# An MLP over sixteen token tiles, worked in five blocks of 2, 4, 4, 4 and 2 tiles instead of four blocks of 4

## The reference

```
hs = layernorm(x)                                 # H=512 channels of C=4
o  = attention(rat_read(hs, attn_read_w, 3))
hs = rat_write(hs, o, attn_wod_w, attn_wab_w, attn_du_w)       # "a" of a tile
mlp_in = rat_read(hs, mlp_read_w, 2)              # 2 x 512 per token, normalised
gate = mlp_in[..., :H] @ mlp_in_w[0].T            # 512 -> M=2048
up   = mlp_in[..., H:] @ mlp_in_w[1].T            # 512 -> 2048
y = silu(gate) * up
hs = rat_write(hs, y, mlp_wod_w, mlp_wab_w, mlp_du_w)          # "w" of a tile
x = x + hs
x = x + low_rank_experts(layernorm(x))                         # "e" of a tile

def rat_write(res, y, ...):       # 632 outputs: 512 out, 8 delta_low, 112 gates
    out, delta_low, A_logit, B_proj, B_skip = y @ [wod; wab].T
    delta = softplus(delta_low @ du_w.T)
    A_bar = exp(-delta * softplus(A_logit))
    return res * A_bar + out * B_full(A_bar, delta, B_proj, B_skip)
```

## Time and profile before

| | us |
|---|---|
| median of 3 runs (1856.93 to 1860.12) | 1858.18 |
| the profiled execution, its own time | 1859.11 |
| its span in the trace | 1857.3 |
| mix stage: from 643.6 to the end | 1213.7 |
| of it, before the first up step | 119.8 |
| the four blocks | 246.0, 290.0, 272.5, 212.4 |
| after the last down step | 73.0 |
| PE busy, whole span | 1648.2 |
| DVE busy, whole span | 1173.0 |

### The profile page before, as it was taken

One profiled execution on the slowest core, in us unless ns is written; L12 is line 12 of the kernel. 1 busy time (PEld: TensorE's weight loads), 2 busy tenths in 40 slices (PEclk: granted clock), 3 DMA queues, 4 the chain that ended last, 5 costly groups with the idle time before them and its releaser, 6 DMA issues.

```text
span 1857.3 us, 23597 instructions
## 1 busy us (share of the span) xinstructions
PE 1648.2 (89%) x8854; PEld 1138.3 (61%) x8854; DVE 1173.0 (63%) x1873; ACT 794.4 (43%) x1486; POOL 267.6 (14%) x243
## 2 busy tenths in 40 slices
PE   6799999999999866899898999897999998999865
PEld 5565655666666535677566677455677565775543
DVE  6678755888888657254355647637458455555577
ACT  1333336888887634455224444223444322331221
POOL 1235332334320000200002000003000002000000
PEclk7899999999999976799898999998999999999988
DMA  7376567878775252566473666554565544665721
GB/s 301 114 266 239 209 172 232 242 205 243 213 195 119 71 203 96 187 223 205 147 236 127 228 214 202 173 164 169 190 234 196 191 161 149 222 200 173 252 79 68
DMA packets 117221, 348.69 MB, mean 188 GB/s; under 512 B 16226, under 2 KB 33250, under 8 KB 101876
## 3 DMA queue, kind: packets, MB, share of 16 engines
q1 hardware_dynamic: 117108, 347.19, 57.6%
HBM read 271.37 MB, written 75.76 MB: 187 GB/s over the span
## 4 chain that ended last, share of the span: by engine, by line
PE 65%; DVE 22%; ACT 6%; issue 4%; DMA 1%; POOL 1%; SPq 0%; DVEq 0%; ACTq 0%
PE ps L1365 15%; PE ps L1377 11%; PE ps L396 6%; PE ps L820 4%; PE ps L1280 4%; PE ps L807 4%; PE ps L843 4%; PE ps L1323 3%; PE ps L1265 3%; PE ps L1308 3%; ACT a_p L922 3%; PE ps L1335 2%; DVE m_A L1438 2%; PE ps L369 2%; DVE m_A L1469 2%
## 5 line engine op out<-in xcount | busy, mean ns | idle before, releaser
L1365 PE MATMUL ps<-m_yhi,m_win 128*128 128x512 f32 x1024 | 352.9, 413 | 0.0
L1377 PE MATMUL ps<-m_wod,m_hT 128*128 128x512 f32 (+1 forms) x1024 | 312.2, 454 | 8.0 <-DVE m_hT L1563 8.0
L1377 PEld LDWEIGHTS ps<-m_wod,m_hT 128*128 128x128 f32 x1024 | 173.6, 201 | 152.0 <-issue 151.5
L1365 PEld LDWEIGHTS ps<-m_yhi,m_win 128*128 128x128 f32 x1024 | 195.4, 191 | 49.2 <-issue 5.1
L864 DVE TENSOR_REDUCE a_negmax<-ps 128x1 f32<-128x640 f32 (+7 forms) x176 | 180.6, 1026 | 59.6 <-PE ps L810 58.7
L1365 PE MATMUL ps<-m_ylo,m_win 128*128 128x512 f32 x512 | 203.9, 398 | 0.0
L922 ACT ACTIVATE a_p<-ps,a_negmax 128x128 f32<-128x128 f32 (+7 forms) x256 | 188.8, 750 | 30.4 <-DVE a_negmax L864 28.0
L820 PE MATMUL ps<-ident,a_p 128*128 128x128 f32 x1152 | 157.5, 275 | 1.4 <-DVE a_pT L877 1.2
L1595 ACT ACTIVATE m_turned<-ps 128x512 f32<-128x512 f32 x128 | 74.0, 593 | 187.8 <-PE ps L1265 187.7
L807 PE MATMUL ps<-a_k,a_q 128*128 128x512 f32 (+3 forms) x384 | 124.2, 403 | 17.1 <-ACT a_p L922 15.3
L820 PEld LDWEIGHTS ps<-ident,a_p 128*128 128x128 f32 x1152 | 123.7, 141 | 3.3 <-DVE a_pT L877 1.9
(11 more groups left out here) (202 smaller groups left out, 2730.4 us busy)
## 6 DMA issues: line engine op xcount, KB each, us to landing
m_win<-mlp_in_split SPq DMA_DIRECT2D x128, 512.0 KB, 4.2
m_wod<-in_wod2T SPq DMA_DIRECT2D x128, 316.0 KB, 3.1
m_wod<-in_wod1T SPq DMA_DIRECT2D x64, 316.0 KB, 3.1
p_xT<-in_xT SPq DMA_DIRECT2D x16, 1024.0 KB, 9.1
p_x<-in_x SPq DMA_DIRECT2D x16, 1024.0 KB, 10.5
a_q<-qk_split SPq DMA_DIRECT2D x64, 256.0 KB, 6.4
a_k<-qk_split SPq DMA_DIRECT2D x128, 128.0 KB, 7.0
mlp_in_split<-a_w_two SPq DMA_DIRECT2D x32, 512.0 KB, 3.0
```

Of the source, the lines that this page charges most:

```text
L1365: m = nc.tensor.matmul(bank_of("m", blk, step), win[s][:, wl, ic, :], y[:, k, :], start=(ic == 0 and p3 == 0), stop=(ic == HCH - 1 and p3 ...
L1377: m = nc.tensor.matmul(ps[:, b, 0:cn], hT[:, k, P * q:P * q + P], w2[s][:, c0:c0 + cn], start=(k == 0), stop=(k == MCH - 1))
```

## The change

The same 16 tiles are put in five blocks of 2, 4, 4, 4 and 2. In the first and the last block an up step streams 256 columns instead of 512, with the same 12 weight tiles and the same 512 KB, and there is one round of 16 down steps. So there are 160 up steps and 128 down steps, where there were 128 and 128. Two tiles' `a` run ahead of the first block, and two lanes' buffers are dropped. All `a`, `w`, `e` and `t` get new places: in the first block four `a` are 10 steps apart, in the next block 18, then 16; `w` and `e` of tile 10, 11, 12, 13 begin 16 and 6 steps before the last block and 6 and 20 steps after its start (it has 48).

```diff
+BLOCKS = [(0, 1), (2, 3, 4, 5), (6, 7, 8, 9), (10, 11, 12, 13), (14, 15)]
+ROUNDS = [[tuple(range(q, q + 2)) for q in range(0, len(tiles), 2)] for tiles in BLOCKS]
+NF = len(BLOCKS[0])
...
-        A_BASE = {i: 64 * (i // TB - 1) + (11 * (i % TB) if i < 2 * TB else 16 * (i % TB) - 13.3) for i in range(TB, NT)}
-        W_BASE = {i: 64 * (i // TB) + 48 + 16 * (i % TB) for i in range(NT - TB)}
-        W_BASE.update({12: 240, 13: 242, 14: 256, 15: 258})
-        E_BASE = {**W_BASE, 13: 245.5, 15: 261}
+        START = [sum(32 + MCH * len(ROUNDS[b]) for b in range(blk)) for blk in range(MBLK + 1)]
+        A_BASE = {i: START[BLOCK_OF[i] - 1] + {1: -8 + 10 * PLACE_OF[i], 4: 4 + 18 * PLACE_OF[i]}.get(
+            BLOCK_OF[i], 16 * PLACE_OF[i] - 13.3) for i in range(NF, NT)}
+        W_BASE = {i: START[BLOCK_OF[i]] + 48 + 16 * PLACE_OF[i] for i in range(NT)}
+        W_BASE.update({0: START[1] - .4, 1: START[1] + 27, 10: START[4] - 16, 11: START[4] - 6, 12: START[4] + 6,
+                       13: START[4] + 20, 14: START[5], 15: START[5] + 2})
+        E_BASE = {**W_BASE, 15: W_BASE[15] + 3.5}
+        T_AT = [-2.5 + .1 * k if not blk else START[blk] - (6.5 - .8 * k if blk == 1 else 8.5 - k)
+                for blk in range(MBLK) for k in range(RD2 * HCH)]
...
-                        m = nc.tensor.matmul(bank_of("m", blk, step), win[s][:, wl, ic, :], y[:, k, :],
+                        m = nc.tensor.matmul(bank_of("m", blk, step)[:, 0:width_of(blk)], win[s][:, wl, ic, :],
+                                             y[:, k, 0:width_of(blk)],
                                              start=(ic == 0 and p3 == 0), stop=(ic == HCH - 1 and p3 == 2))
...
-            for e in range(2):
-                q = 2 * q2 + e
-                for c0, cn, b in ((0, H, 2 * e), (H, ABW, 2 * e + 1)):
-                    m = nc.tensor.matmul(ps[:, b, 0:cn], hT[:, k, P * q:P * q + P], w2[s][:, c0:c0 + cn],
+            for q in tiles:
+                for c0, cn, b in ((0, H, 0), (H, ABW, 1)):
+                    m = nc.tensor.matmul(bank_of("d", blk, q, b)[:, 0:cn], hT[:, k, P * q:P * q + P],
+                                         w2[s][:, c0:c0 + cn],
...
+            w = width_of(blk)
+            V.tensor_scalar(yraw[k % 2][:, 0:w], bank_of("t", blk, k)[:, 0:w], gam2[:, k:k + 1], bet2[:, k:k + 1],
```

More of the change, by code:

```diff
@@ L265, in program @@
         ylo = sb("m_ylo", [P, RD2 * HCH, BLK], F32R)
-        hT_place = place[0]
         hT = sb("m_hT", [P, MCH, BLK])
         assert place[0] <= attend_end, place[0] - attend_end
[L271 to L283, removed]
+        place[0] = yhi_place
+        f_oT = [oTt[:, :, :], sb("m_first_oT1", [P, HCH, P])[:, :, :]]
         place[0] = y2_place
@@ L1142, in program @@
                 quarter[what, i, q] = len(quarter)
+            if part in ("read", "down"):
+                assert quarter[what, i, q] == len(used_quarters), (what, i, q)
+                used_quarters.append((what, i, q))
         stored = {}
@@ L1164, in program @@
         for what, i, part, q in order:
-            first = what == "a" and i < TB
+            first = what == "a" and i < NF
             pair = 2 if first and i % 2 else 4
@@ L1190, in program @@
             if what == "m" and part >= 32 and (part - 32) % MCH == 0:
-                for b in range(4):
-                    one.plan(("d", i, (part - 32) // MCH, b), b)
-            if what == "m" and (i, part) == (NBLK - 1, 63):
+                for q2 in ROUNDS[i][(part - 32) // MCH]:
+                    for b in (2 * (q2 % 2), 2 * (q2 % 2) + 1):
+                        one.plan(("d", i, q2, b % 2), b)
+            if what == "m" and (i, part) == (MBLK - 1, 31 + MCH * len(ROUNDS[MBLK - 1])):
                 one.banks = [6, 7, 0, 1, 2, 3]
@@ L1684, in mlp_act @@
                 return
-            q2, k = divmod(step - 32, MCH)
+            r, k = divmod(step - 32, MCH)
             if k == MCH - 1:
-                for e in range(2):
-                    q = 2 * q2 + e
-                    act.wait_ge(wod2_mm, wod2_count(blk, q2, k, e))
-                    act.wait_ge(hs_ready, nth("sum", "w", (blk - 1) * TB + q) if blk else nth("sum", "a", q))
-                    S.activation(outs2[q][:, :], ps[:, 2 * e, :], ACT.Copy).then_inc(emptied[2 * e], 1)
+                for q in ROUNDS[blk][r]:
+                    act.wait_ge(wod2_mm, wod2_count[blk, r, k, q])
+                    if before_place(blk, q):
+                        act.wait_ge(hs_ready, nth("sum", *before_place(blk, q)))
+                    S.activation(outs2[q][:, :], bank_of("d", blk, q, 0), ACT.Copy).then_inc(
+                        one.sem(("d", blk, q, 0)), 1)
         def mix_act():
```

138 lines of the change are left out of this document (74 added, 64 removed).

## The result

The changed kernel takes 1883.08 us (median of 4 runs, 1880.58 to 1892.77) against 1859.15 for the kernel before in the same session: 1.0139 times as long (95% interval 1.0101 to 1.0177). It is slower by 1.4%; forecast were 1850 and a range of 1830 to 1872. The profiled execution took 1881.85, its span is 1880.1.

A forecast was written before the change was run, and what follows sets the result against it. PE paces the blocks; at both ends a tile's chain through DVE and ACT does. 71 us in front, 941 of PE work and 132 of waits, 62 behind make 1206 against 1213.7: -8, so 1850 us, range 1830 to 1872.

The forecast's parts named there:

- Front end, -49: Ahead of the first up step: two tiles fewer and shorter waits save 49 us, 40 at the low end.
- Back end, -11: After the last down step: earlier gates save 5.4 us, fewer DVE additions with their softmaxes 6; between -7 and -13.
- PE's work, +34: In the blocks: narrow up matmuls at 0.128 us (+9), more `a` (+15), `w` and `e` (+8), turns (+2).
- The rival of the weight loads: Weight loads pace narrow up matmuls at 0.19 us (1898) or 0.21 us (1915) instead of 0.128; chance 0.03 together.
- Waits in the blocks, +18: Narrow steps cover less of each tile's DVE and ACT work, so PE's waits in the blocks grow 18 us net.
- The 8.0 us wait and its clock loss go (-11): First block: PE's wait at the first down step for DVE's last product into hT disappears, saving 11 us.
- 4 us a tile for 3.2 tiles: First block: each `a` outlasts its cover of narrow steps and other PE work, adding 13 us of waits.
- +16, +3 and -3: Last-block waits for tiles 11 to 13, +16; one more block transition, +3; one less `e` colliding with an `a`, -3.
- the ring through hs0: First block: turns, load, scaling and sum take about as long as PE's 10 steps and one `a`, 25.8 us.
- DVE pacing the narrow blocks: Rival: DVE stretches do not fit between narrow steps; gain gone from 6 us a tile, 1870 at 8; chance 0.19.
- More gained: Rival: narrow blocks hide DVE's stretches beside PE's `a` and `w` work, waits +0 or less, 1832 us; chance 0.24.
- Transfers: Rival: 512 KB in each 1.54 us narrow step paces the blocks, +17 us, 1867; chance 0.06.

The follow-up runs named there:

- e3: Changed kernel with the four state-sum passes of tiles 2 to 5 on a quarter of their columns; 1869.3 us.
- e4: Changed kernel with each up matmul of the first block streaming its 256 columns twice; 1910.6 us.
- e11: Changed kernel with each up matmul of the last block streaming its 256 columns twice; 1913.5 us (one run).
- e1: Changed kernel with up-matmul weight transfers of 256 KB instead of 512 KB in the two blocks of 2 tiles; 1887.8 us.
- e6: Changed kernel with norm and scaling moved earlier for tiles 2 to 5, and the sums of tiles 3 and 5 behind the next hT product; 1876.8 us.

## Why the prediction was wrong

**Front end, -49.** Right: 119.8 to 73.2 is -46.6. (The low end that the prediction gives for it, -40, comes to -42 by its own terms, and 60.1 / 3 is 20.0.) **Back end, -11.** It was -7.7, and both terms were there: the gates began 6.7 us after the last down step instead of 11.4, 4.7 less where 5.4 was forecast, and from there to the end it was 3.0 less where 6 was forecast. DVE paces, as said: PE's turn of tile 14 waited 22.3 us for it.

**PE's work, +34.** Right in sum: busy time grew by 35.8. The matmul was dearer in the forecast (0.128) than on the chip (0.117), some 8 us less over 768 of them; the lower clock took about that back. The row that I leaned on, 0.116 for 272 columns, was the better guide than the difference that I added to it. The rival of the weight loads is out. The rule of the Trainium skill, TensorE: Matmul & The Clock Gate, that a weight load overlaps matmuls only in another row group ("The mechanism") would have made it 0.21; the trace disagrees, at 0.117. The same section names a background weight buffer as a second case in which a load goes ahead of matmuls in flight, and the rival left that out.

**Waits in the blocks, +18: the step that failed.** In the forecast's terms the blocks were to hold 941 of work and 132 of waits and lower clock. They take 1098.0, of which some 933 is work with the faster matmul, so 165 is the rest, 51 above the 114 of before, of which 41 are waits and some 10 the lower clock. The last block came out right (140 forecast, 141.2), and so did the size of its waits, some 5 us a tile, but two of the three long ones are at the experts' weighted product (L1554) behind the state sum, a link that the forecast did not name, and only one at a bank: the size was right in part by luck. The first was not: 156 forecast, 178.0 measured, and these 22 us are most of the miss of 31 in the mix stage (1206 forecast, 1236.5). The sharpest error is one term: "The 8.0 us wait and its clock loss go (-11) if the new place of the last `a` keeps clear of the last products": it did not keep clear. Tile 5's sum stands at step 30, between the last two products, just as tile 6's did before; the engines' lists show it. Instead of -11 that gave +3.8, 15 us of the 33 that separate 51 from 18.

The other 18 us: "4 us a tile for 3.2 tiles", +13, was nearly right in size, for the up steps of the first block hold 14.6 us of waits where there were none; but they are not one wait a tile, they are spread over the links of the chain (3.81 and 2.49 at tile 3's turn, 1.66 and 0.72 for attention outputs, and others). The four later blocks hold 22.1 us more of waits than the three before (80.1 against 58.0), where the forecast had 16 (+16, +3 and -3), another 6. And some 10 us are the lower clock behind all these waits, for which the step had no term: in the first block's up steps alone 0.94 instead of 0.99 over 102 us, by my estimate 5 us. Last, of the ring through hs0 the step says that it "shows only if something else is late", and puts it at nothing: something else was late, and the load of tile 5's state is a link of that chain.

**The rivals.** What happened is the one with 0.19, DVE pacing the narrow blocks, beyond its 1870. e3, e4 and e11 show its mechanism, with two corrections: it is the length of a chain through the tile's load, ACT and DVE, and not DVE's busy time (51% of the first block); and its own condition, 6 us a tile, is not met in the first block's up steps (14.6 / 3.2 is 4.6), so that the time beyond 1870 owes as much to the -11 that did not come and to the clock. More gained (0.24) had the largest chance after the forecast and nothing speaks for it. Transfers: out by e1.

What stays open: what a second buffer beside the one hs0 would give back, which no run tried, and what decides how much lower clock follows a wait, some 10 of the 51 us.

## What to carry to other kernels

Halving a step halves the cover of everything that is placed by steps: before such a change, write down for each long pass (here 7 us of DVE) which short operation stands behind it and how many us of the other engine's work lie ahead, in the new steps. Where a wait shows an engine held by a short product behind a long pass, put the long pass behind it, but only where its own consumer is far enough off in us: here it was worth 11.6 us in wide steps. Moving one link of a chain that is late as a whole gives back little (1.4 and 2.5 us here) and can move the wait; look first for the link that cannot start earlier, here a load into a buffer that is still in use.

## What was not expected of the hardware

The same wait does not always bring the lower clock. Both executions below are of the same instructions on PE, the changed kernel's and e6's at the same place in the fourth block, in windows of PE that both begin 13.5 us ahead of the same delta matmul; before it PE waited 2.17 us in both. The first lines are the changed kernel's, the second e6's:

```profile
1450.00:1460.00 10.00, 10.00 (x41) 7.36 (x41) 7.14 (x8) 3.37 (x3) 0.00 (x0) 1.00 0.48 146
1460.00:1470.00 10.00, 7.83 (x32) 5.68 (x32) 9.71 (x13) 5.12 (x10) 0.11 (x1) 1.00 0.93 341
```

```profile
1441.20:1451.20 10.00, 10.00 (x42) 7.36 (x41) 7.14 (x8) 3.37 (x3) 0.00 (x0) 1.00 0.54 148
1451.20:1461.20 10.00, 7.83 (x26) 5.59 (x25) 9.65 (x13) 5.08 (x10) 0.16 (x1) 0.83 0.82 311
```

The granted clock stayed at 1.00 (2.4 GHz) in one and was 0.83 on the mean in the other, which therefore spent part of the window at 1.2 GHz. The third, fourth and last blocks take 269.5, 248.7 and 141.2 us in one and 272.2, 252.9 and 144.4 in the other: such differences make 10.1 us, with PE's idle time the same within 0.3 us. Runs of one kernel spread by up to 14 us here, so the blocks' waits were compared and not the totals alone. What decides it these runs don't show.
